# Attention scores of the second pass over 64 operand rows instead of 33, the added rows of the keys zero

## The reference

```
qkvo = W x + b;  q, k, v = three parts, 12 heads of 32 channels
attn = softmax(q k^T / sqrt(32)) over 1024 x 1024 pixels, per head
res  = attn v + depthwise 5x5 conv(v)
out  = W_proj (res * o) + b_proj
```

## Time and profile before

| what | value |
|---|---|
| median of 3 runs | 11385.86 us (11383.32 to 11387.95) |
| the profiled execution | 11378.4 us |
| its span, first to last instruction | 11376.6 us |
| mean granted clock of TensorE | 0.813 |
| TensorE busy | 8954.9 us, 79% |
| VectorE busy | 7592.8 us, 67% |
| POOL / ACT busy | 3956.4 us, 35% / 3900.4 us, 34% |

### The profile page before, as it was taken

One profiled execution on the slowest core, in us unless ns is written; L12 is line 12 of the kernel. 1 busy time (PEld: TensorE's weight loads), 2 busy tenths in 40 slices (PEclk: granted clock), 3 DMA queues, 4 the chain that ended last, 5 costly groups with the idle time before them and its releaser, 6 DMA issues.

```text
span 11376.6 us, 106333 instructions
## 1 busy us (share of the span) xinstructions
PE 8954.9 (79%) x36120; PEld 4204.5 (37%) x36120; DVE 7592.8 (67%) x5637; ACT 3900.4 (34%) x4474; POOL 3956.4 (35%) x1678
## 2 busy tenths in 40 slices
PE   6985888588886888768896788858898688877556
PEld 2223333343334433344333433334333443334433
DVE  3127667866677667776668666686677766687892
ACT  1113344333333333432443334333333323343331
POOL 0004333433334333442334333343234423343560
PEclk8665888788886898778886888868898789878657
DMA  1006444744457444664447534474445744466782
GB/s 34 4 19 207 154 144 166 245 172 143 140 179 241 156 141 152 216 200 149 148 148 244 193 129 156 163 244 164 136 148 190 225 155 141 153 225 195 246 267 65
DMA packets 717974, 1876.29 MB, mean 165 GB/s; under 512 B 258897, under 2 KB 274641, under 8 KB 717265
## 3 DMA queue, kind: packets, MB, share of 16 engines
q1 hardware_dynamic: 717392, 1869.00, 49.4%
HBM read 1772.03 MB, written 71.04 MB: 162 GB/s over the span
## 4 chain that ended last, share of the span: by engine, by line
PE 57%; DVE 25%; issue 7%; ACT 5%; DMA 2%; DVEq 2%; SPq 1%; ACTq 1%; POOL 0%; POOLq 0%
DVE R L1630 11%; PE ps L902 9%; PE ps L875 8%; PE ps L748 8%; PE ps L855 7%; PE ps L984 7%; DVE ps L1620 6%; PE ps L886 4%; ACT R L1174 3%; PE ps L1069 3%; DVE nmx L1560 2%; PE ps L1052 2%; PE ps L891 1%; PE ps L957 1%; PE ps L981 1%
## 5 line engine op out<-in xcount | busy, mean ns | idle before, releaser
L1345 POOL TENSOR_TENSOR R<-R 128x1024 f32<-128x1024 f32 x1536 | 3659.8, 2383 | 5546.8 <-DVE ps L1620 5546.8
L1630 DVE TENSOR_TENSOR_SCAN R<-R,ps 128x1024 f32<-128x1024 f32 x1536 | 3508.1, 2284 | 440.1 <-ACT R L1233 334.1
L1233 ACT ACTIVATE R<-R,negA 128x1024 f32<-128x1024 f32 x1536 | 1749.9, 1143 | 2946.0 <-DVE R L1630 2908.6
L984 PE MATMUL ps<-ident,R 128*128 128x128 f32 x12288 | 2068.0, 327 | 588.1 <-POOL R L1345 547.5
L984 PEld LDWEIGHTS ps<-ident,R 128*128 128x128 f32 x12288 | 1746.1, 171 | 1512.1 <-POOL R L1345 753.3
L1620 DVE TENSOR_TENSOR ps<-R 128x1024 f32<-128x1024 f32 x1536 | 1993.1, 1298 | 109.3 <-DVE R L1630 4.7
L1560 DVE TENSOR_REDUCE nmx<-ps 128x2 f32<-128x1024 f32 x768 | 936.4, 1219 | 850.1 <-PE ps L855 843.9
L902 PE MATMUL ps<-R 128*128 128x512 f32 x2400 | 1258.6, 648 | 0.0
L1174 ACT ACTIVATE R<-ps 128x1024 f32<-128x1024 f32 x768 | 785.8, 1023 | 1325.6 <-PE ps L875 1325.6
L875 PE MATMUL ps<-R 33*128 33x512 f32 x3072 | 1048.0, 765 | 173.9 <-ACT R L1174 88.4
L855 PE MATMUL ps<-R 32*128 32x512 f32 x3072 | 939.4, 690 | 198.9 <-DVE nmx L1560 164.6
(11 more groups left out here) (154 smaller groups left out, 5749.7 us busy)
## 6 DMA issues: line engine op xcount, KB each, us to landing
R<-bc_scratch SPq DMA_DIRECT2D x3072, 512.0 KB, 4.7
R<-in_x SPq DMA_DIRECT2D x72, 512.0 KB, 6.8
out<-R SPq DMA_DIRECT2D x72, 512.0 KB, 5.2
R<-shift_scratch SPq DMA_DIRECT2D x48, 640.0 KB, 7.4
R<-R SPq DMA_DIRECT2D x192, 128.0 KB
R<-out SPq DMA_DIRECT2D x48, 512.0 KB, 8.4
R<-in_w_qkvo SPq DMA_DIRECT2D x32, 576.0 KB, 6.7
rows_scratch<-R SPq DMA_DIRECT2D x24, 512.0 KB, 7.3
```

The source lines that it names most:

```text
L984: mm = pe.matmul(ps[:, 4 + b // 4, (b % 4) * P:(b % 4 + 1) * P], state[i % HELD][:, b * P:(b + 1) * P], ident[:, :], start=fresh and i % G ...
L1233: act.activation(decay[i % len(decay)], dt[:, c, :], ACT.Exp, scale=negA[:, col:col + 1]).then_inc(a_sb.h, 1)
L1345: pool.tensor_tensor(state[i % HELD], state[i % HELD], rows_c[slot], ALU.mult).then_inc(hc_sb.h, 1)
L1630: v.tensor_tensor_scan(h, a, b, 0.0, ALU.mult, ALU.add).then_inc(h_sb.h, 1)
```

## The change

T's matmuls take rows 0 to 63 and 64 to 127 instead of 0 to 32 and 64 to 96. The rows in between (33 to 63 and 97 to 127) must not add anything, so those of the keys are zero: `k2[1]` is filled with zeros once at the start, `k2[0]` once an image at event "vz", ahead of the fill of `vpad`, since other stages write into its place. The same rows of `q2` hold whatever lay there. VectorE waits for the sixth projection (`qk_sb`) before it fills. SP, which writes the rows of `k2`, waits for the end of this fill instead of the first scores.

```diff
@@ SP, event "q2", group 0
-                        sp.wait_ge(s_ps.h, s_ps.at(img, 1))
+                        sp.wait_ge(vz_sb.h, vz_sb.at(img, 1))
                         for pair in range(2):
                             for row in (HD, HD + 64):
                                 sp.dma_start(k2[pair][row:row + 1, :], ones[0:LB, :]).then_inc(q2_in.h, 16)
@@ TensorE, event "T"
                     for j in range(2):
-                        rows = slice(64 * j, 64 * j + HD + 1)
+                        rows = slice(64 * j, 64 * j + 64)
                         mm = pe.matmul(ps[:, bank + j, :], k2[pair][rows, kb * P:(kb + 1) * P],
                                        q2[g][pair][rows, qh * HALF:(qh + 1) * HALF], start=True, stop=True)
@@ VectorE, event "vz"
                 if kind == "vz":
+                    v.wait_ge(qk_sb.h, qk_sb.at(img, 6))
+                    v.memset(k2[0], 0.0)
                     v.memset(vpad, 0.0).then_inc(vz_sb.h, 1)
@@ VectorE, before the first event
             v.memset(negm[:, :], 0.0)
+            v.memset(k2[1], 0.0)
             v.memset(ones[:, :], 1.0)
```

## The result

The changed kernel takes 11097.2 us in the median of 4 runs (11087.0 to 11105.3), against 11384.6 us before: a ratio of 0.9747, 95% interval 0.9730 to 0.9764, 287 us less. The profiled execution took 11096.4 us.

The account below looks back on a forecast made before the run. No engine was full overall, but TensorE led the chain (57%), full at the low clock in image 0's T passes. Terms -154 - 110 + 7 = -257 us gave 11129 us from the 11385.9 us median, range 11070 to 11222.

Parts of the forecast that it names:

- 33 of 64 rows in T is what keeps the prologue low: Image 0's T passes: the throttle sees how many TensorE rows work, so 33 rows hold the clock at 0.50.
- Zeros in the operand do not count against an instruction: TensorE throttle: rows holding zeros count as working, since depthwise taps with diagonal weights, 127 zeros of 128, hold clock 1.00.
- Prologue, 154 us: Image 0's three T passes: 51.3 us saved per group by the higher clock, 154 us in all, bounds 145 and 165.
- two small terms: Deductions per prologue T pass: 5 us low-clock start, 2.5 lost; one return to low clock behind the middle wait, 1.7 lost.
- Loop, 110 us: The 21 T phases of the seven later images: 110 us saved, four fifths of 137, bounds 50 and 150.
- The itemised stretches: One loop image's low-clock T work, 46.5 us, 45% saved: 21 us an image, 125 in six, 12 for image 1.
- Fills, 7 us: Zero fills of k2 on VectorE, 0.91 us each: seven on the loop's path, one at the start; +7 us, bounds 0 and 10.
- The waits, nothing: VectorE's new wait for the sixth q/k projection and SP's wait moved to the vpad fill: no cost.
- Rival B: Only the prologue gains; the loop's low stretches stay, begun by waits or taken over by VectorE: 11219 us, chance 0.13.
- C: The clock does not move, as the throttle ignores rows or zero keys; only fills remain: 11393 us, chance 0.11.
- D: T's pair of 64-row matmuls stops overlapping, 650 us more: 11779 us, slower, chance 0.02.
- The signs named at the end of the prediction: Prologue T: clock 1.00, events 1.13 us, pass near 77 us; line 875 near 665 ns; loop 0.93 or more; fill 0.91 us.

Follow-up runs that it names:

- the fills alone: Changed kernel with T's matmuls back at 33 rows, the two fills and SP's moved wait kept: 11392.8 us, ratio 1.0008.
- the row counts: Changed kernel with T's matmuls over 48 rows each, 11148.8 us, ratio 0.9782, or over 40 rows, 11198.2 us, ratio 0.9830.
- the fill of 0.001: Changed kernel with both k2 fills writing 0.001 instead of 0: 11100.8 us, ratio 0.9750.
- push and cover: Kernel before, image 0 only: six unused 128-row matmuls behind each group's turned maxima, T event ahead of the middle wait issued four times: 11212.1 us, ratio 0.9850.
- the kernel with the push: Kernel before, 33 rows, no fills; in image 0 six unused 128-row matmuls behind each group's turned maxima: 11292.6 us, ratio 0.9920.
- the covers: Changed kernel, image 0 only: five unused matmuls at T's start, T event issued four times at the middle wait, four matmuls at the end: 11083.4 us, ratio 0.9730.
- the one at the start of a pass: Changed kernel plus five unused 128-row matmuls behind the turned maxima of each group, in all images: 11131.8 us, ratio 0.9771.
- the cover at the end of a pass: Changed kernel with five unused matmuls at every T pass's start, plus four before the transposes opening the next S pass: 11130.0 us, ratio 0.9770.

## Why the prediction was right

11129 us were forecast, 11097 us measured; the saving was 287 us where the sum had 257. By the steps of the prediction:

- *33 of 64 rows in T is what keeps the prologue low.* Right as to what the edit does, shown by the fills alone (0.50) and by the row counts. "Zeros in the operand do not count against an instruction": right for the keys, shown by the fill of 0.001. But it is half of the mechanism. What the prediction left out is that winning the high clock takes more than holding it: 33 rows stand at 1.00 in the same pass once the clock is high and no wait intervenes (push and cover). The loop's T events of 1.13 us were a sign of it, and I read them as the transposes' doing. (The 2.08 us beside them are from the prologue; the loop has such events too, the first of a pass among them.) In the loop both may be at work; this was not separated there.
- *Prologue, 154 us.* From its first T event to the division behind it a pass took 123.8, 124.1 and 125.2 us before, and takes 71.7, 73.0 and 71.7 now: 156.7 us less. The first scan shows 152.0, since the first pass starts 4.7 us later. In the first pass it is 236.18 to 307.87 us, where 72.5 were forecast. Inside, two small terms erred against each other: the start at the low clock took 6 us, not 5, and the return to it behind the wait (1.7) did not come in group 0 (1.00 from 242 to 306); it came in group 1 alone, whose pass is 1.3 us longer. The idle time there is 3.19 us, forecast 3.1.
- *Loop, 110 us.* This is the term that was mis-sized. The itemised stretches came to 137 and I took four fifths, for VectorE's sake. With the fills in, 131.0 us are gone from first to last scan; the kernel with 64 rows beside the scans alone, again with the fills, shows 127. The undiscounted sum, less some 6 for the fills, is 131. That the two meet so closely is in part luck. In the image that I had itemised, the first T events of the three passes start at 4054.14, 4299.79 and 4541.95 us and that of the next image at 5398.81; now they start at 3873.89, 4116.70, 4355.85 and 5198.39. So from one start to the next 2.8, 3.0 and 14.3 us are gone, the last with the fill in it, where the stretches gave 2.6, 6.1 and 12.2. Group 1, where VectorE was busy 6.21 of 7 us, gave half of its share, and the stretch from group 2 on gave more than its own. A discount was due in one place, and I took it everywhere.
- *Fills, 7 us.* 8 us by the medians of the kernel with the fills alone, within an interval from 2 us less to 19 more; one fill takes 912 ns in the trace, forecast 0.91 us.

The fill of `k2[0]`, by its line:

```profile
L1557 DVE MEMSET R<- x8: 912/912/912, 130.0 to 9033.3; 128x1024 f32 x8
```

- *The waits, nothing.* Nothing was seen of them in the timeline: in the loop S runs at 3737.51, ahead of the fill at 3739.25. In the prologue SP's first row starts at 132.31 us, just as the fill of `vpad` ends (131.14 + 1.14), and the first T event that needs it comes at 236.18.
- *Rival B* (prologue alone) fell by the kernel with 64 rows beside the scans only, *C* by the measured clock, *D* by T events of 1.13 us; the 0.2 us of fixed cost in D's price stands in no row, and nothing here measured it. The signs named at the end of the prediction showed: 1.00 with 1.13 us, a pass near 77 us with its end (236.18 to 312.05, where the next transposes start), line 875 at 677 ns where 665 was forecast, T passes of the loop at 0.95, and a new fill of 0.91 us.

The rule of the Trainium skill that was weighed (TensorE: Matmul & The Clock Gate, "What's actually happening") asks how busy TensorE has been. Occupied time alone is not that measure: in the kernel with the push TensorE is busy 50 of 50 us at 0.50, behind the wait in the middle, having been busy 31.73 of 32 us at 1.00 ahead of it. That the clock falls behind a wait of 3.19 us in this pass does agree with the rule.

What stays open: whether 33 rows would hold the clock in the loop, if only it were never lost there; what starts image 0's first T pass up to some 9 us earlier or later from one kernel to the next; and whether the cover at the end of a pass does anything beside the scans.

## What to carry to other kernels

Where a matmul stage is full and yet at the low clock, compare the rows of its matmuls with those of stages at 1.00. Here a contraction widened with zero rows made no matmul longer, and one fill of the operand an image bought it. Look also at what lets the clock fall. Where the stage had 33 rows, waits of 4.3 us in front of it and 3.2 us in its middle cost the whole stage, and covering both with work that adds nothing to the result was worth as much as the rows. Where it had 64 rows, the covers gave some 4 us in image 0, and the one at the start of a pass lost 28 us beside the scans, where other work queued behind them.

## What the hardware showed that was not expected

- The same work stands at either level, depending on what came before: the same stage of 33-row and 128-row events, with TensorE full, stood at 1.00 for 32 us and, after a wait of 3.19 us, at 0.50 for 50 us.
- Behind that same wait in the first pass, 40 rows were back at 1.00 after 13.5 us, and with 64 rows the clock did not fall in two of the three passes.
- Rows between 33 and 64 count by degrees, not in strips of 32, and the first few count most: by the ratios, the step from 33 to 40 rows is worth 203 us, that from 48 to 64 rows 40 us.
